# Attention and feed-forward block on one core: weights transposed on VectorE, K projected before its transform, and the middle part's x transposed by DMA

## The reference

```python
# attention by autocorrelation, 16 heads of 16
Q, K, V = heads(layernorm(x) @ wq), heads(ctx @ wk), heads(ctx @ wv)
corr = irfft(rfft(Q) * conj(rfft(K)), n=L)          # along time
top_vals, top_idx = top_k(corr, 4)
w = softmax(top_vals)
out = sum_i w[i] * V[(t - top_idx[i]) % 16]          # rolled inside the head
x = x + out @ wo
# feed-forward with simulated quantization
x_q = quantize_a16(layernorm(x))                     # scale from the maximum over the whole tensor
hidden = gelu(x_q @ quantize_w8(W_in) + b_in)
out = quantize_a16(hidden) @ quantize_w8(W_out) + b_out   # again one maximum over all of hidden
return x + out
```

## Time and profile before

| | before |
|---|---|
| median of 3 runs (lowest, highest) | 1168.51 us (1166.54, 1168.67) |
| the profiled execution | 1167.71 us, of it 1166.1 us span |
| attention part, up to the first matmul of the middle | 0 to 679.3 us |
| middle part | 679.3 to 903 us |
| last part | 911.2 us to the end |
| TensorE busy | 1107.7 us, 95% of the span |
| VectorE busy | 1068.8 us, 92% |
| ScalarE busy | 908.8 us, 78% |
| GpSimd busy | 493.3 us, 42% |
| granted TensorE clock, mean | 0.98 |

### The profile page before, as it was taken

How to read it: one execution, slowest core, us unless ns; L and a number is a source line. 1 busy time by engine, 2 the same in 40 slices (tenths; PEclk the granted TensorE clock), 3 DMA queues, 4 the chain that set the end, 5 groups by cost and what they waited for, 6 DMA issues and landing times. The chain is left out here.

```text
span 1166.1 us, 30895 instructions
## 1 busy us (share of the span) xinstructions
PE 1107.7 (95%) x9803; PEld 882.7 (76%) x9803; DVE 1068.8 (92%) x2883; ACT 908.8 (78%) x1510; POOL 493.3 (42%) x855
## 2 busy tenths in 40 slices
PE   5799999999999999999999579999999799999998
PEld 4689999999999999999998434444444688888886
DVE  5899999999999999999999479999998799999998
ACT  3567777777777777777787368888888788888885
POOL 3467777777777777777776330000000000000000
PEclk9999999999999999999999789999999899999999
DMA  7223333333333333333332025555557799999995
GB/s 251 82 83 111 111 112 111 111 111 111 110 111 110 109 110 110 110 110 110 110 110 65 37 109 216 229 239 234 216 216 311 285 328 341 338 338 333 337 334 204
DMA packets 85403, 207.37 MB, mean 178 GB/s; under 512 B 7856, under 2 KB 44080, under 8 KB 81200
## 3 DMA queue, kind: packets, MB, share of 16 engines
q1 hardware_dynamic: 84208, 204.97, 49.4%
q10 hardware_dynamic: 1088, 1.05, 0.3%
HBM read 122.11 MB, written 83.89 MB: 177 GB/s over the span
## 5 line engine op out<-in xcount | busy, mean ns | idle before, releaser
L603 PE MATMUL bank<-wout,arena 128*128 128x256 f16 x2048 | 239.5, 274 | 7.9 <-DVE arena L1221 6.1
L623 ACT ACTIVATE arena<-bank 128x512 f16<-128x512 f32 (+1 forms) x256 | 146.6, 598 | 117.9 <-PE bank L422 84.5
L603 PEld LDWEIGHTS bank<-wout,arena 128*128 128x128 f16 x2048 | 196.1, 98 | 52.9 <-DVE arena L1228 17.1
L573 PE MATMUL bank<-store_x,win 128*128 (+1 forms) x1024 | 222.8, 381 | 4.9 <-ACTq L749 4.9
L573 PEld LDWEIGHTS bank<-store_x,win 128*128 128x128 f16 x1024 | 100.5, 98 | 127.0 <-issue 7.1
L1228 DVE SCALAR_TENSOR_TENSOR arena<-arena,wout_rel 128x512 f16<-128x512 int16 x256 | 183.0, 746 | 2.1 <-ACT arena L787 1.0
L745 ACT ACTIVATE arena<-bank,b_in_sb,z_scale 128x512 f32<-128x512 f32 x192 | 147.4, 777 | 17.4 <-PE bank L573 11.7
L623 ACT ACTIVATE arena<-arena 128x512 f16<-128x512 f32 (+1 forms) x192 | 119.9, 627 | 42.7 <-POOL arena L830 39.7
L634 ACT ACTIVATE arena<-arena 128x256 f32<-128x256 f32 x256 | 139.9, 603 | 8.6 <-POOL arena L825 8.6
L782 ACT ACTIVATE arena<-arena,one 128x1536 int16<-128x1536 f32 x64 | 100.7, 1575 | 40.1 <-DVE arena L1228 33.9
L1189 DVE TENSOR_REDUCE hmax<-arena 128x1024 f32 (+1 forms) x96 | 111.3, 1211 | 4.3 <-ACT arena L745 4.3
(11 more groups left out here) (116 smaller groups left out, 2237.6 us busy)
## 6 DMA issues: line engine op xcount, KB each, us to landing
hidden_scratch<-arena SPq DMA_DIRECT2D x32, 1536.0 KB, 5.0
arena<-hidden_scratch SPq DMA_DIRECT2D x64, 768.0 KB, 6.7
arena<-in_x SPq DMA_DIRECT2D x64, 256.0 KB, 2.8
arena<-in_ctx SPq DMA_DIRECT2D x64, 256.0 KB, 3.0
arena<-in_ctx_turned SPq DMA_DIRECT2D x64, 256.0 KB, 2.6
x_scratch<-arena SPq DMA_DIRECT2D x64, 256.0 KB, 2.0
arena<-x_scratch SPq DMA_DIRECT2D x32, 512.0 KB, 6.3
out<-arena SPq DMA_DIRECT2D x32, 512.0 KB, 3.5
```

Of the source, the lines that this page charges most:

```text
L573: last = nc.tensor.matmul(bank[b][:, :], win16[:, c, f * P:(f + 1) * P], rhs_of(c), start=s == 0 and c == 0, stop=s == 1 and c == DC - 1)
L603: last = nc.tensor.matmul(bank[m * 2 + k // 2][:, k % 2 * D:(k % 2 + 1) * D], gbuf[:, s, f, k * P:(k + 1) * P], wout16[:, f, :], start=f = ...
L623: nc.scalar.activation(dst, src, ACT.Copy).then_inc(S[done], 1)
```

## The change

1. The mixing weights no longer go through TensorE. GpSimd multiplies them by the inverse sum and a two-column mask (`spread_weights`), and VectorE transposes blocks of 32 x 32 straight into `mt` (`turn_weights`). For this the host permutes time and head columns (`by_head`). `spread_heads`, `mixing`, `mix_out` and `weigh` go; `invert_sum` gets one more small instruction.
2. K is projected first, from the transposed ctx that V uses too (`project_k`), copied to SBUF as f32 (`take_k`), and transformed after that (`dft_k`). The untransposed ctx is no longer loaded; `dft_context`, `high_cf` and `low_cf` go.
3. `turn_ln2` and `take_turned` go: the normalized x1 is stored as it is. In the middle part the two rounded halves are transposed by a DMA on SP's queue, one per quad, into a ring of three buffers `xt`, which `hidden` reads. Two of these lie in free room of the arena, the third in `hidden_in[3]`, whose first load moves behind the last gelu.
4. Steps are reordered on every engine, `attend` and `project_out` run a step later, `vt` has four buffers, and loops are unrolled.
5. In the last part the waits for the stores of hidden move from before `to_int` to the first writes of `gbuf`.

```diff
+            def dft_k(p):
+
+                pe.wait_ge(S["kf_out"], p + 1)
                 wait(pe, S["terms_done"], p)
                 for r in range(2):
-                    for c in range(DC):
-                        for k, (i, j) in enumerate(PARTS):
...
+                    for b in range(2):
+                        last = nc.tensor.matmul(bank[3][b * NF:(b + 1) * NF, r * D:(r + 1) * D], dft[:, r * NF:(r + 1) * NF], kf[:, b, :],
+                                                start=True, stop=True)
                 last.then_inc(S["k_done"], 1)
...
+                if active(t, 5):
+                    attend(t - 5)
                 if active(t, 1):
+                    project_v(t - 1)
+                    project_k(t - 1)
+                if active(t, 3):
+                    inverse(t - 3)
+                if active(t, 5):
+                    project_out(t - 5)
+                if active(t, 1):
+                    project_q(t - 1)
+                    dft_k(t - 1)
                 if active(t, 0):
+                    dft_norm(t)
...
+            def spread_weights(p):
+                pool.wait_ge(S["wsum_done"], p + 1)
+                pool.wait_ge(S["rsum_done"], p + 1)
+                wait(pool, S["mt_out"], p)
+                nc.gpsimd.tensor_tensor(wmask, wmix.unsqueeze(2).broadcast_to([P, 4, 2, HD]),
+                                         rsum_of.unsqueeze(3).broadcast_to([P, 4, 2, HD]), ALU.mult).then_inc(S["w2_done"], 1)
...
+            def turn_weights(p):
+
+                if p == 0:
+                    dve.wait_ge(S["mt_zero"], 1)
+                dve.wait_ge(S["w2_done"], p + 1)
                 wait(dve, S["ot_done"], p)
+                for i in range(4):
+                    part = slice(32 * i, 32 * i + 32)
+                    last = V.transpose(mt.rearrange("p c b l -> p (c b) l")[part, :, part], wmask.rearrange("p g j r -> p g (j r)")[part])
+                last.then_inc(S["mt_out"], 1)
...
+            def turn_x(q):
+                sp.wait_ge(S["xlo_done"], q + 1)
+                wait(sp, S["b_mm"], (q - 2) * FC)
+                sp.dma_start_transpose(xt[q % 3].rearrange("p s n c t -> p (s n c) t"), xq[:, q].rearrange("p s k -> p (s k)")).then_inc(s_xt[q % 3], 16)
+
+            for q in range(2):
+                turn_x(q)
+            for q in range(QUADS - 2):
+                turn_x(q + 2)
+                store_hidden(q, q % 2)
...
+            for q in range(QUADS):
+                pe.wait_ge(s_xt[q % 3], 16 * (q // 3 + 1))
                 for f in range(FC):
                     pe.wait_ge(S["b_gelu"], q * FC + (f + 1))
-                    hidden(q, f, f).then_inc(S["b_mm"], 1)
+                    hidden(q, f).then_inc(S["b_mm"], 1)
...
             def high(q, f):
+                if isinstance(q, int) and q == 0 and f in (1, 7):
+                    act.wait_ge(s_h_st[f // 6], 16 * (QUADS // 2))
```

More of the change, by code:

```diff
@@ L54, in constants @@
     table = np.zeros((P, C_ALL), np.float64)
+    time = t % HD * NH + t // HD
     angle = 2 * np.pi * np.outer(t, f) / P
@@ L404, in _, with dft_norm @@
             PARTS = ((0, 0), (1, 0), (0, 1))
-            def dft_context(p, n):
-                m = n % 2
-                wait(pe, s_c_in[m], landed(p, n))
-                wait(pe, S["cf_low"], p)
-                for c in range(DC):
-                    for b in range(2):
-                        last = nc.tensor.matmul(freq(1)[:, c, :, b, :], cin[m][:, b, c * P:(c + 1) * P], dft, start=True, stop=True)
-                last.then_inc(S["front_cf"], 1)
-            def dft_norm(p, n):
-                wait(pe, S["ln1"], p + 1)
+            def dft_norm(p):
+                pe.wait_ge(S["ln1"], p + 1)
                 wait(pe, S["fx_low"], p)
@@ L533, in step @@
                     spread_w_in_scale(1)
[L534 to L537 removed]
+                if active(t, 5):
+                    attend(t - 5)
                 if active(t, 1):
[L539 to L554 removed]
+                    project_v(t - 1)
[7 more added lines that the diff above has]
+                    dft_k(t - 1)
+                if active(t, 0):
+                    dft_norm(t)
+            for t in range(PAIRS + 5):
+                step(t)
             pe.wait_ge(S["top_done"], PAIRS)
@@ L742, in _ @@
-            act.wait_ge(S["x_scale"], 2)
+                    normalize2(t - 6)
+                if active(t, 0):
+                    high_ct(t)
+            for n in (0, 3, 1, 2):
+                high_w(n)
+            for t in range(PAIRS + 6):
+                step(t)
             def gelu(dst, b, f, done):
@@ L874, in _, with step @@
-            steps(pool, step, 6)
+            def spread_weights(p):
[4 more added lines that the diff above has]
+                                         rsum_of.unsqueeze(3).broadcast_to([P, 4, 2, HD]), ALU.mult).then_inc(S["w2_done"], 1)
+            def step(t):
+                if active(t, 0):
+                    scale1(t)
+                if active(t, 4):
+                    spread_weights(t - 4)
+                if active(t, 2):
+                    add_terms(t - 2)
+                if active(t, 3):
+                    take_shift(t - 3)
+                if active(t, 0):
+                    low_ct(t)
+                if active(t, 2):
+                    low_cs(t - 2)
+                if active(t, 5):
+                    scale2(t - 5)
+                if active(t, 4):
+                    low_ot(t - 4)
@@ L1141, in step @@
                     round_w_out()
-            steps(dve, step, 6)
+            for t in range(PAIRS + 6):
+                step(t)
             sc = [0]
```

590 lines of the change are left out of this document (234 added, 356 removed).

## The result

The changed kernel is slower. Its median is 1190.77 us (four runs, 1189.38 to 1192.01) against 1168.5 us for the kernel before: a ratio of 1.0197, 95% interval 1.0182 to 1.0211. The forecast was 1136 us, faster. The profiled execution has a span of 1187.6 us against 1166.1.

What follows compares the result with a forecast made beforehand. TensorE was taken to pace the attention part (9.68 us a pair), VectorE 4.5% behind. 1167.7 - 34.8 (steady steps) + 1 (drain) + 4.0 (first transpose) - 2.9 (last part) = 1135.0 profiled, so 1136 us median; range 1116 to 1200.

Steps and rivals of the forecast that it cites:

- VectorE's sum: Attention part, VectorE's work per pair: 9.24 - 1.33 + 1.15 = 9.06 us, between 8.7 and 10.5.
- ScalarE and GpSimd ... Neither becomes the bound: Attention part: ScalarE loses two copies, GpSimd gains spread_weights (0.45 us) for about 8.0 us a pair, at most 8.7.
- the three rivals: dft_k's columns don't overlap (chance 0.13); DMA transposes pace the middle part (0.24); VectorE's transposes or another loop are slow (0.11).
- the third: Attention part: VectorE's block transposes take 0.60 us each, VectorE needs 10.5 us, total 1219; chance 0.11 with another loop.
- TensorE, per pair: Attention part: 9.68 us less 0.88 and 0.90, plus dft_k's pitch, gives 9.10 us, between 8.80 and 9.70.
- X: Pitch of dft_k on TensorE: five slots, 1.07 us, plus 0.13 for the change of shape, 1.20; bounds 0.90 and 1.80.
- the four transposes: VectorE's block transposes in the attention part: 0.25 us each, +1.00 a pair, sized from top_values at 0.20 each.
- Ends of the attention part: Start left as it is, within 3 us; drain after the last dft_norm, 51.4 us before, taken as +1.
- Drain and first transpose: Between attention and middle parts: +1 us for the drain, +4.0 for the first DMA transpose, taken as 5 us.
- The middle part: TensorE stays at 6.91 us a quad; DMA transposes are hidden and cost nothing, if up to 2.6 times a copy.
- The second rival: Middle part paced by DMA transposes, 10.6 us an issue on SP against 6.91, +118 us, total 1254; chance 0.24.
- Into the last part: to_int starts at once behind the scale instead of waiting for the last store: -2.9 us, the last part moving whole.

Runs made afterwards that it cites:

- experiment 1: The changed kernel with weigh_hot moved later on VectorE, behind low_fx and invert_sum: 1145.27 us, ratio 0.9816 to the kernel before.
- experiment 2: The changed kernel with one_hot moved to the end of VectorE's step and weigh_hot to the head of the next: 1149.91 us, ratio 0.9851.
- experiment 3: The changed kernel with low_ot ahead of scale2 on GpSimd, VectorE's order untouched: 1180.99 us (one run).
- experiment 7: On top of experiment 1, only two of the four block transposes of turn_weights: 1128.1 us (one run).
- experiment 6: On top of experiment 1, dft_k's two loops swapped, so its products go batch first: 1146.95 us (one run).
- experiment 4: The changed kernel without the middle part's DMA transposes, hidden reading the rounded x as it lies: 1184.98 us, ratio 1.0144.
- experiment 5: On top of experiment 1, each quad's DMA transpose issued twice, TensorE waiting for both: 1253.73 us (one run).
- experiment 8: On top of experiment 1, ScalarE's wait for all stores of hidden put back ahead of to_int: 1148.86 us (one run).

## Why the prediction was wrong

**The step that failed** is VectorE's sum and the line under it, "ScalarE and GpSimd ... Neither becomes the bound". It added durations of VectorE as if they were its own affair. It placed `low_ot` on GpSimd in time, and found that it ends before it is wanted, but never asked what VectorE runs in those 1.16 us. `weigh_hot` had cost 0.39 before and was carried over at that; it took 1.34, and the step 10.11 us in place of 9.10. Experiments 1 and 2 move the instruction and bring it to 0.41 and 0.42, experiment 3 moves the other partner and hits another instruction. None of the three rivals held this; the third ("slow transposes on VectorE or another loop") had VectorE as the bound, by another cause.

The Trainium skill states this rule ("SBUF — State Buffer", SBUF: two separate sides): VectorE and GpSimd share a pair of ports as an exclusive lock, which a VectorE instruction with two SBUF inputs and a GpSimd one that reads SBUF take for the whole instruction, the later one standing still. For `low_ot` the trace agrees: 1.34 us, until 0.28 us after its end. It also agrees in what is spared: L964, with one operand in PSUM, keeps its 0.68 us under `low_ot` in experiment 1. For L756 it doesn't: this GpSimd instruction reads SBUF too and lasts 0.71 us, but L921 and L941, which start 0.54 and 0.34 us into it, keep their 0.41 and 0.17 us. So the lock isn't held for the whole of every GpSimd instruction; when L756 lets go, no run here shows.

**TensorE, per pair.** Right: 9.10 was forecast, and 9.12 is what TensorE takes when nothing holds it (experiment 7). `dft_k` itself has a pitch of 1.01, but `project_q` ahead of it rose from 1.31 to 1.40 and `dft_norm` behind it from 0.89 to 0.99, so that it costs some 1.2 in all, as X did, which had 0.13 in it for the change of shape. The 8.92 in the expectations of experiments 6 and 7 leaves these two out. Passes do run beside each other, in another way than X assumed (experiment 6).

**VectorE, per pair, without the clash.** 9.06 was forecast; experiment 1 has a step of 9.35 with VectorE busy 98.4% of it. The mis-sized term is the four transposes: 1.28 us by pitch (309.36 to 310.64) in place of 1.00. They last 300 ns each, some 0.31 by pitch; the row chosen for them, `top_values`, has 0.20 by pitch. With 1.28 the sum is 9.34. That this meets 9.35 so closely is in part luck: the sum is of busy time, of which experiment 1 has 9.20 us a step; the other 0.15 us are short gaps between instructions. So even without the clash the forecast of 9.10 was too low by 0.25, 14 us over 55 steps, and VectorE, 0.23 above TensorE's 9.12, is the limit.

**GpSimd.** `spread_weights` takes 0.40 for 0.45. Its own time stayed below the bound.

**Ends of the attention part.** Off both ways: the start was put at nothing (within 3 us) and is 8.4 us shorter up to pair 8 (6.5 to 9.7 in experiments 1 to 6 and 8); why is open. Drain and first transpose were +5 and are +8.1, of which 4.0 is the transpose (experiment 4, forecast 4.0; its landing took 3.94 us for 5) and some 4 the drain, forecast at 1.

**The middle part.** Right on what decides: hidden but close, 92% of the DMA queue. The second rival's 10.6 us an issue did not come (1.6 us on SP as a rule, at most 3.0), nor the 1309 ns a block that was set beside it: sixteen blocks landed in 3.7 us. The part is 1.2 us longer, and experiment 4 puts all of it down to the transposes (222.75 us without them, as before) and to the lower granted clock of the beginning. The prediction's 221.04 us was read from a row of 1016 of the 1024 matmuls.

**Into the last part.** 2.9 forecast; from the last gelu to the first `output` it is 5.40 against 8.23 us, 2.8 less. The size is right in part by luck: the moved wait is worth 1.7 of it in experiment 8, and the other 1.1 would have come without it, as the last store lands sooner.

**The sum for experiment 1,** the change without its accident: 1135.0 was forecast for the profiled execution, and it took 1145.0, of it 1143.2 us span. The steady steps give 55 x 0.33 = 18 us, the start 9.7, the handoff 2.8 and the rest 0.5; the drain with the first transpose takes 7.0 and the middle 1.2. The change is good for 1.8% here; the place of one instruction in VectorE's order hid it.

## What to carry to other kernels

When VectorE or GpSimd is within a few per cent of the bound, lay their two timelines over each other before adding up durations: each VectorE instruction with two SBUF operands that a change slides under a GpSimd instruction like `low_ot` (512 elements a partition) costs what is left of that one. The one on two elements did no harm, and others were not tried. After a change, look first for a line whose duration changed while its shape did not. The cure is a place or two in either engine's order, but look at who lies there, since the clash moves along.

## What the runs showed of the hardware

- A VectorE product of 256 elements a partition with two SBUF operands that starts during a GpSimd instruction of 1.15 us on 512 elements ends 0.28 us after it (305.57 for 305.29; 302.19 for 301.91). With VectorE first, GpSimd's instruction grows from 0.71 to 0.86 us.
- An 8-element VectorE instruction is hit too (0.17 to 0.67 us), one with an operand in PSUM or with a single one is not. Under GpSimd's 0.71 us power of two elements none is hit (0.41 and 0.17 us).
- A DMA transpose of 16 blocks of 128 x 128 f16 lands in 3.7 us and takes some 2.6 us of all 16 DMA engines, 2.1 times a copy at the stores' rate; its issue holds SP's queue for some 1.6 us (1.3 to 3.0) where the store's takes 0.34.
- A VectorE transpose on 32 partitions x 128 elements takes 300 ns, against 280 for `top_values` of 128 elements (by pitch 0.31 against 0.20 us).
- Eight f32 passes of 256 columns on 64 of the array's columns take 1.02 us in either order: they start in pairs within 0.02 us, four pairs 0.21 to 0.26 us apart. The block ahead of them and the block behind them, which use all columns, are each 0.1 us longer than between neighbours that use all columns too.
